# Cross-attention's transposes: from TensorE to 32x32 blocks on VectorE and a round trip through device memory, with a two-step pipeline and doubled projection weights

## What is computed

```python
x = x + _L0_attn_ref(_layernorm(x), ...)                 # causal self-attention, 32 heads of 16
x = x + _L0_xattn_ref(_layernorm(x), ctx_4096, ...)      # cross-attention, below
x = x + _L0_ffn_ref(_layernorm(x), ...)                  # 512x512 linear, 4-bit weights, bias
```

```python
# cross-attention: 32 query heads and 8 key/value heads of width 128; kv_len = 256
kv = jnp.concatenate([context, latents], axis=1)
q = rms_norm((latents @ Wq)..., q_norm_w); k = rms_norm((kv @ Wk)..., k_norm_w); v = (kv @ Wv)...
scores = jnp.einsum('bhgqd,bhkd->bhgqk', qg, k) * scale
probs = jax.nn.softmax(scores, axis=-1)
out = jnp.einsum('bhgqk,bhkd->bhgqd', probs, v)
return out.reshape(...) @ Wo
```

## Time and profile before

| | |
|---|---|
| median of three runs | 1114.6 us |
| the profiled execution's own time | 1114.33 us |
| its span in the trace (first to last instruction) | 1112.2 us |
| TensorE matmuls busy | 1050.4 us (94%) |
| VectorE, ScalarE, GpSimd busy | 757.1, 611.9, 358.5 us |
| mean granted TensorE clock | 0.982 of full |
| bytes moved by DMA | 31.73 MB, mean 29 GB/s |

### The profile page before, as it was taken

One profiled execution on the slowest core, in us unless ns is written; L12 is line 12 of the kernel. 1 busy time (PEld: TensorE's weight loads), 2 busy tenths in 40 slices (PEclk: granted clock), 3 DMA queues, 4 the chain that ended last, 5 costly groups with the idle time before them and its releaser, 6 DMA issues.

```text
span 1112.2 us, 19358 instructions
## 1 busy us (share of the span) xinstructions
PE 1050.4 (94%) x6436; PEld 902.8 (81%) x6436; DVE 757.1 (68%) x1561; ACT 611.9 (55%) x2324; POOL 358.5 (32%) x460
## 2 busy tenths in 40 slices
PE   6788888778999999999999999999999999999998
PEld 5666666547888888888888888888888888888886
DVE  6788888756557756665666576657666665667774
ACT  2666666525555655555555555555555555555551
POOL 4622333033114312431432143114313331433443
PEclk9899999878999999999999999999999999999999
DMA  5000010003001100110011011001100110010002
GB/s 180 21 10 9 9 66 10 1 3 126 6 1 58 39 1 2 57 38 0 19 38 38 0 57 38 0 0 57 38 0 0 57 38 0 11 37 1 1 1 76
DMA packets 8935, 31.73 MB, mean 29 GB/s; under 512 B 1600, under 2 KB 1600, under 8 KB 6720
## 3 DMA queue, kind: packets, MB, share of 16 engines
q1 hardware_dynamic: 8896, 31.23, 8.0%
HBM read 29.13 MB, written 2.10 MB: 28 GB/s over the span
## 4 chain that ended last, share of the span: by engine, by line
PE 64%; POOL 7%; DVE 3%; ACT 2%; issue 1%; POOLq 0%; DVEq 0%
PE ps_q L76 15%; PE ps_y L76 14%; PE ps_kv L76 13%; PE ps_s L76 7%; PE ps_o L76 7%; PE ps_pT L1210 4%; POOL wq_lo L876 3%; POOL wkv_lo L876 2%; PE ps_q L1216 2%; ACT p L957 1%; PE ps_kv L1221 1%; POOL q_rms L884 1%; DVE neg_max L1042 1%; POOL k_rms L884 1%; DVE wkv_hi L1035 0%
## 5 line engine op out<-in xcount | busy, mean ns | idle before, releaser
L957 ACT ACTIVATE p<-ps_s,bias,q_rms 128x256 f32<-128x256 f32 x256 | 141.3, 560 | 117.1 <-DVE bias L1046 116.3
L1068 DVE TENSOR_TENSOR pT_lo<-ps_pT,pT_hi 128x512 fp32r<-128x512 f32 x128 | 82.5, 686 | 75.6 <-ACT pT_hi L983 75.4
L993 ACT ACTIVATE oT_hi<-ps_o 128x512 fp32r<-128x512 f32 x64 | 38.3, 598 | 139.2 <-PE ps_o L76 139.2
L882 POOL TENSOR_TENSOR k_rms<-k_mean,rms_eps 128x2 f32<-128x2 f32 x64 | 19.6, 306 | 283.9 <-ACT k_squares L964 283.9
L76 PE MATMUL ps_y<-wo_hi,oT_hi 128*128 128x512 f32 x256 | 106.5, 416 | 0.0
L76 PE MATMUL ps_q<-wq_hi,xT_hi 128*128 128x512 f32 x256 | 101.1, 395 | 2.5 <-POOL wq_lo L876 2.5
L76 PE MATMUL ps_q<-wq_hi,xT_lo 128*128 128x512 f32 x256 | 101.9, 398 | 0.0
L76 PE MATMUL ps_y<-wo_hi,oT_lo 128*128 128x512 f32 x256 | 101.4, 396 | 0.0
L76 PE MATMUL ps_q<-wq_lo,xT_hi 128*128 128x512 f32 x256 | 100.9, 394 | 0.0
L76 PE MATMUL ps_y<-wo_lo,oT_hi 128*128 128x512 f32 x256 | 100.7, 393 | 0.0
L971 ACT ACTIVATE q_sb<-ps_q 128x512 f32<-128x512 f32 x64 | 38.3, 599 | 100.8 <-PE ps_q L76 99.5
(11 more groups left out here) (210 smaller groups left out, 3316.1 us busy)
## 6 DMA issues: line engine op xcount, KB each, us to landing
raw_wq<-in_x_wq SPq DMA_DIRECT2D x8, 1024.0 KB, 4.8
raw_wo<-in_x_wo SPq DMA_DIRECT2D x8, 1024.0 KB, 4.9
raw_wkv<-in_x_wkv SPq DMA_DIRECT2D x8, 512.0 KB, 3.3
ctx_raw<-in_ctxT SPq DMA_DIRECT2D x8, 256.0 KB, 2.6
out<-raw_wq SPq DMA_DIRECT2D x8, 256.0 KB, 2.0
x<-in_x SPq DMA_DIRECT2D x1, 1536.0 KB, 9.8
raw_wq<-in_a_wq SPq DMA_DIRECT2D x2, 512.0 KB, 6.0
raw_wq<-in_a_wo SPq DMA_DIRECT2D x1, 1024.0 KB, 4.7
```

The source lines that it names most:

```text
L957: act.activation(p[:, g, :], ps_s[g // 2][:, g % 2 * KV:(g % 2 + 1) * KV], ACT.Exp, bias=bias[:, g:g + 1], scale=q_rms[:, g:g + 1], accum_ ...
L993: act.activation(oT[0][:], ps_o[:].rearrange("p (g s) -> p g s", g=XG), ACT.Copy).then_inc(o_hi, 1)
L1068: dve.tensor_tensor(pT[1][:, t], ps_pT[t][:].rearrange("p (g s) -> p g s", g=XG), f32(pT[0][:, t]), ALU.subtract).then_inc(pT_lo, 1)
```

## The change

- TensorE no longer transposes `p`, `q` and `k`. VectorE transposes them by blocks of 32x32 (`p_blocks`, `qk_blocks`), SyncE stores the blocks to a scratch tensor in device memory and loads them back with the blocks in their places (`qk_raw`, `pT_raw`): one store and four loads each for queries with keys, and for probabilities. Each of the four loads fills 32 partitions.
- The high halves are then taken from these tiles in SBUF by ScalarE, and the low halves of the queries and of the probabilities by GpSimd (before, VectorE took them). The low half of the keys stays on VectorE.
- The pipeline is deeper: TensorE's step is now `scores(s)`, `project_keys_values(s + 2)`, `project_output(s - 2)`, `project_queries(s + 2)`, `values(s - 1)`.
- `wkv` and `wq` have two pairs of buffers; their splitting is spread over the steps `b = 0` to `5`. Half of `wo_lo` is computed by VectorE in step `b = 1`.
- All 64 steps are written out; there is no loop. The end is ordered anew: rows 0 to 3 of the linear layer run inside the last two steps.

```diff
         def _(sp):
...
+            def queries_keys(s):
+                sp.wait_ge(k_blocked, s + 1)
+                sp.wait_ge(q_blocked, s + 1)
+                wait(sp, qT_lo, s)
+                scratch = io["qk_scratch"][s % 2]
+                sp.dma_start(scratch, qk_blocks[:].rearrange("p j x c -> p (j x c)")).then_inc(qk_stored, 16)
+                wait(sp, kT_lo, s)
+                sp.wait_ge(qk_stored, 16 * (s + 1))
+                quadrants = scratch.rearrange("(i r) (j x) -> j r i x", i=4, j=4)
+                for j in range(4):
+                    sp.dma_start(qk_raw[R * j:R * j + R].rearrange("p i x c -> p i (x c)"), quadrants[j]).then_inc(qk_loaded[s % 4], 16)
+            def probs(s):
+                sp.wait_ge(p_blocked, 2 * s + 2)
...
+                sp.dma_start(scratch, p_blocks[:].rearrange("p m g c -> p (m g c)")).then_inc(p_stored, 16)
...
+                sp.wait_ge(p_stored, 16 * (s + 1))
...
+                for j in range(4):
+                    sp.dma_start(f32(pT_raw[s % 2][R * j:R * j + R].rearrange("p i t x -> p i (t x)")),
+                                 quadrants[j]).then_inc(p_loaded[s % 4], 16)
...
+            for s in range(STEPS):
+                j, b = divmod(s, B)
+                if s + 1 < STEPS:
+                    queries_keys(s + 1)
+                probs(s)
+                if b == 3 and j < LAST:
...
+                    load(raw_wo, "x_wo", wo_in, j + 1)
+                if b == 4 and j + 2 < XKVH:
...
+                    load(raw_wkv, "x_wkv", wkv_in, j + 2)
+                if b == 6 and j + 2 < XKVH:
...
+                    load(raw_wq, "x_wq", wq_in, j + 2)
...
+                if b == 7 and j + 1 == LAST:
+                    for t in range(2):
+                        for g in range(8):
+                            sp.dma_start(scale[16 * g:16 * g + 16, t, :],
...
         def _(pool):
+            def queries_low(s):
+                pool.wait_ge(qT_hi, s + 1)
+                pool.tensor_tensor(qT[1][:].rearrange("p g (i c) -> p g i c", i=4),
+                                   qk_raw[:, :, 0:XG, :].rearrange("p i g c -> p g i c"),
+                                   f32(qT[0][:]).rearrange("p g (i c) -> p g i c", i=4), ALU.subtract).then_inc(qT_lo, 1)
+            def probs_low(s):
+                pool.wait_ge(pT_hi, s + 1)
+                raw = pT_raw[s % 2][:].rearrange("p i t x -> p (i t x)")
+                pool.tensor_tensor(raw, f32(raw), f32(pT_hi_sb[:].rearrange("p i t x -> p (i t x)")),
+                                   ALU.subtract).then_inc(pT_lo, 1)
...
+            for s in range(STEPS):
+                j, b = divmod(s, B)
+                if j < LAST and b in (2, 3):
+                    weights_low(wkv[(j + 1) % 2], raw_wkv, (2 * b - 4, 2 * b - 3), wkv_hi, wkv_lo, j + 1)
+                if j < LAST and b in (4, 5):
+                    weights_low(wq[(j + 1) % 2], raw_wq, (2 * b - 8, 2 * b - 7), wq_hi, wq_lo, j + 1)
+                if s:
+                    probs_low(s - 1)
+                if s + 2 < STEPS:
+                    k_rms_step(s + 2)
+                if s + 1 < STEPS:
+                    queries_low(s + 1)
+                if b == 1:
+                    weights_low(wo, raw_wo, (2, 3), wo_hi, wo_lo, j + 1)
+                if s + 2 < STEPS:
+                    q_rms_step(s + 2)
...
         def _(act):
+            for s in range(STEPS):
+                j, b = divmod(s, B)
+                if s >= 2:
+                    output_high(s - 2)
                 exps(s)
+                if s:
+                    probs_high(s - 1)
+                if s + 2 < STEPS:
+                    keys_values(s + 2)
+                if s + 1 < STEPS:
                     queries_keys_high(s + 1)
+                if s + 2 < STEPS:
+                    query_sums(s + 2)
...
         def _(dve):
+            def probs(s, h):
...
+                wait(dve, p_stored, 16 * s)
+                dve.wait_ge(p_ok, 2 * s + h + 1)
+                dve.transpose(p_blocks[:, :, two, :], p[:, two, :].rearrange("p g (m r) -> p m g r", r=R)).then_inc(p_blocked, 1)
...
+            def queries_blocked(s):
+                dve.wait_ge(q_ps, s + 1)
+                wait(dve, qk_stored, 16 * s)
+                dve.transpose(qk_blocks[:, :, 0:XG, :].rearrange("p j x c -> p x j c"),
+                              ps_q[:].rearrange("p (g j r) -> p g j r", g=XG, r=R)).then_inc(q_blocked, 1)
...
+            for s in range(STEPS):
+                j, b = divmod(s, B)
                 biases(s)
+                if s >= 2:
+                    output_low(s - 2)
+                probs(s, 0)
+                probs(s, 1)
+                if s + 2 < STEPS:
+                    values_low(s + 2)
+                if s >= 2:
+                    residual(s - 2)
+                if b == 1:
+                    output_weights(j)
+                if s + 1 < STEPS:
+                    keys_low(s + 1)
+                if s + 2 < STEPS:
+                    keys_blocked(s + 2)
+                    queries_blocked(s + 2)
```

More of the change, by code:

```diff
@@ L780, in cross_attention_and_linear @@
         p = sb("p", [P, XG, KV])
-        pT = split("pT", [P, 2, XG, S])
+        p_blocks = sb("p_blocks", [P, 8, XG, R])
+        pT_hi_sb = sb("pT_hi_sb", [P, 4, 2, XG * R], F32R)
+        pT_raw = [sb(f"pT_raw{i}", [P, 4, 2, XG * R], F32R) for i in range(2)]
         oT = split("oT", [P, XG, S])
@@ L799, in cross_attention_and_linear @@
         ps_q, ps_kv = mem["ps_q"], mem["ps_kv"]
[L800 removed]
         ps_o, ps_y = ps("ps_o"), ps("ps_y")
[L802 to L803 removed]
+        ps_xn = [ps("ps_xn"), ps_kv]
+        ps_f = [ps("ps_f"), ps_q]
         kv_rows = ps_kv[:].rearrange("p (t w) -> p t w", t=2)
@@ L872, in _, with weights_low @@
         def _(pool):
-            def weights_low(w, raw, hi, lo, count):
+            def weights_low(w, raw, rows, hi, lo, count):
                 pool.wait_ge(hi, count)
-                for c in range(C):
+                for c in rows:
                     i = pool.tensor_tensor(w[1][:, c, :], raw[:, c, :], f32(w[0][:, c, :]), ALU.subtract)
@@ L1174, in _, with project_keys_values @@
+            statistics(6)
+            normalised(6)
+            out_row(4)
+            out_row(5)
+            output_low(STEPS - 1)
+            xn_low_row(6)
+            residual(STEPS - 1)
+            statistics(7)
+            normalised(7)
+            out_row(6)
+            xn_low_row(7)
+            out_row(7)
         @block.tensor
         def _(pe):
-            def project_keys_values(s, b, j):
-                wait(pe, kT_lo, s)
-                if not (isinstance(j, int) and j == 0):
-                    pe.wait_ge(wkv_lo, j)
-                rows = slice(b * S, (b + 1) * S)
+            def project_keys_values(s):
+                j, b = divmod(s, B)
+                wait(pe, v_lo, s)
+                wait(pe, k_ok, s)
+                wait(pe, wkv_lo, 2 * j)
+                rows, weight = slice(b * S, (b + 1) * S), wkv[j % 2]
@@ L1298, in build @@
+            xn_transposed(4)
+            xn_transposed(5)
+            project_output(STEPS - 2)
+            linear(4)
+            linear(5)
+            values(STEPS - 1)
+            xn_transposed(6)
+            project_output(STEPS - 1)
+            linear(6)
+            xn_transposed(7)
+            linear(7)
 def build(nc, io):
```

502 lines of the change are left out of this document (236 added, 266 removed).

## The result

The kernel after takes 1157.65 us, median of four runs (1145.42 to 1161.73); the kernel before took 1114.49 us beside it. The ratio is 1.037 (95% interval 1.029 to 1.046): slower, 98 us above the forecast and outside its range. The profiled execution took 1155.22 us, its span 1153.4 us.

The account below looks back on a forecast made before the run. TensorE's own work was taken as the bound, 12.86 us a step. 1114.3 - 101.7 = 1012.6 us, plus 16 + 7 + 6 + 4 + 10 + 4, gave 1059.6, so 1060 us; range 1022 to 1130.

Parts of the forecast that it names:

- The floor of a step: TensorE's own work in a plain step once the transposes go: 12.86 - 1.56 = 11.30 us.
- The four plain chains: GpSimd scores to scores, probabilities, queries and keys, SyncE: each closes within 11.3 us in plain steps, within 2 us of it.
- The weights: Weight loads queued ahead of a store of queries and keys: one us a head, +7 us (0 to 50).
- Rival 4: TensorE's clock drops after waits of 1 to 3 us; 22.6 us a step at half clock; 0.18 with rival 2.
- rival 1: Divisions caught by `probs_low` on GpSimd, weight loads then come through in full: 1118 us (1085 to 1145); chance 0.23.
- 0.1 us of margin: In a plain step the last division starts at 5.3 us, `probs_low` at 5.3 to 5.4, so the division may go first.
- GpSimd's weights against `bias` and divisions in steps 2 to 5, 28 times: GpSimd's weight work holding up VectorE in these steps: +4 us (0 to 15).
- rival 2: SyncE's stores and loads through device memory bound the step, 14 us: 1233 us; decides from 12.1; 0.18 with Rival 4.
- Last head and tail: GpSimd's unpacking, linear layer waiting in the last two steps, last row alone: +10 us (0 to 20).
- the loads of `scale`: Sixteen small loads issued in one step ahead of the next step's queries: 7.4 us of issue less slack, +6 us.
- step `b = 1`: VectorE splits `wo` ahead of `kT_lo`, eight times: step 13.1 instead of 11.3 us, +16 us (0 to 25).

Follow-up runs that it names:

- run 5: Kernel after without most of the later heads' weight loads (stale weights) and without the division of the probabilities: 1063.95 us, ratio 0.955.
- run 1: Kernel after with later heads' weight loads fetching only 64 columns (stale weights), all engine work kept: 1104.93 us, ratio 0.993.
- run 2: Kernel after without VectorE's division of the probabilities by their sums: 1111.26 us, ratio 0.999.
- run 7: Kernel after with all eight rows of the linear layer moved behind the last step: 1140.88 us, ratio 1.023.
- run 9: Kernel after with weights loaded in quarters, scale loads four a step, GpSimd waiting for the divisions and the linear layer last: 1090.43 us, ratio 0.980.
- run 13: As run 9, but the weight quarters are issued by ScalarE into its own queue: 1079.92 us, ratio 0.967.
- run 11: Kernel after with probabilities transposed on TensorE again, weights in quarters and the linear layer last: 1085.60 us, ratio 0.974.

## Why the prediction was wrong, by its steps

**The floor was right.** "The floor of a step is 11.30 us" measured 11.28 in run 5, the transposition 0.71 (taken 0.69), the store of the probabilities 2.7 (2.8), doubled weights 2.8 (2.5). Scores of step 2 start at 285.6 (forecast 287). The four plain chains of the forecast hold within 11.3 us when nothing irregular happens, with the divisions too: step 6 takes 11.3 us in the kernel after, steps 7 and 0 do in run 1.

**The weights: the step that failed first.** "1 MB at 351 GB/s is 3.0 us: the chain of 20 to 21 becomes 23 to 24. One us for a head, 7." Measured 53 (run 1), 7.8 us a head. The rate was the mean of all transfers of the kernel before (31.23 MB in 8.0% of the span); in the window at 618 the stream moved 181 GB/s, in part in pieces of 768 B and 1 KB. The store behind `wo` lands in 7.7 us; the forecast had 2.4 + 3.0. It had left out the four loads of the probabilities issued just ahead: from 618.00 on 0.5 + 1 + 0.375 MB are under way, landed at 628.84. And behind the wait the clock is low: scores 2.93 instead of 1.42 us, keys and values 4.15 instead of 2.88, 2.8 us more at this place. Rival 4 came nearest to this, with waits in each step, and I gave it no price of its own. The forecast's own bound for this term was "0 to 50", just short of what was measured.

**The divisions: the second step that failed, and not where rival 1 had it.** Rival 1, with a chance of 0.23, gave pairs of 2 to 3 us (2.67 and 2.87) and scores waiting for `qT_lo` in steps 4, 5 and 7 (16.5, 13.8, 13.9), and these came. But it expected the catch in plain steps, where the forecast had "0.1 us of margin", and there the good side came out. The rows of a plain step, head 3, `b = 7`:

```profile
664.94 0.62 DVE L1132 TENSOR_SCALAR p<-p,inv 128x256 f32<-128x256 f32 x2
```

```profile
665.32 2.51 POOL L940 TENSOR_TENSOR pT_raw<-pT_raw,pT_hi_sb 128x1024 fp32r<-128x1024 f32 x1 [3.22 <-ACT pT_hi_sb L1045]
```

`probs_low` starts 0.1 us behind the start of the last division, and the pair takes 0.62. Counted over heads 1 to 6 of the kernel after, a division of over 0.6 us (one alone takes 0.31 to 0.39) stands in none of the 18 steps `b = 1, 6, 7`, in 22 of the 24 steps `b = 2` to `5`, and in four of the six `b = 0`, which follow the long step 7; in run 1 it is 21 of the same 24 and none of all others. In `b = 2` to `5` GpSimd has the next head's weights ahead of `probs_low`; they hold up VectorE first (the pair at 597.83, beside them, takes 1.14 us) and change which of the two starts earlier. So the term that was mis-sized is "GpSimd's weights against `bias` and divisions in steps 2 to 5, 28 times: +4. (0 to 15.)": it had no layout of such a step, with `probs_low` behind the weights. Run 1 against run 5 puts the divisions at 41 us with no weights to load, a little of it VectorE's own dividing. No run moves GpSimd's weights elsewhere, so their part is read from these counts and not tested. That a margin of 0.1 us held in every plain step is luck; the layout, summed from durations of other instructions, was not that exact.

The time of rival 1, 1118, was 40 too low, because of its link between the two causes: it let the divisions cost something only by using up the slack of the weights. Run 2 against run 5 shows the weights at 47 us with no division in the way. Its 7.5 us of weights a head, where 7.8 were measured, agree by luck as well: they were reckoned at the full rate and clock. In rival 2 a subtraction is off, 47 us over 64 steps leave 0.8 of the 1.56 and not 0.7; its threshold of 12.1 us is right.

The Trainium skill ("SBUF — State Buffer", section "SBUF: two separate sides") has the exclusive lock that was cited. The traces agree again: 681 ns a division with a free order, 418 with GpSimd held back.

**Last head and tail, +10 us: the third.** From the scores of step 56 to the end the kernel before takes 132.7 us. Without the 11.8 us of transposes in it, and 1.5 less for the deeper pipeline (5.7 - 4.2), that is a floor of 119.4; the forecast adds 6 for the loads of `scale`, 2 for `b = 1` and 10. Measured are 159.6 us in run 5 and 166.3 in the kernel after. In run 5, where heads are bare, the seven steps of head 7 still take 103.3 us, against 79.1 for seven of 11.3. Step 56, with the loads of `scale`, has 6.7 of the 24 (a term of its own in the forecast, 6: right); step 57 3.3, step 60 3.0, and step 62, with the linear layer inside, 11.2. So the term of 10 measures some 33 in run 5 and 40 in the kernel after, where its upper bound was 20. Run 7 gives back 17 by order alone. That "the linear layer waits inside the last two steps" was right in kind; its 4 us were too few. What the other half of the term is, no run shows.

**Too high:** step `b = 1`, 2.0 us taken, 0.6 measured (11.9), 5 us instead of 16. Most of the splitting of `wo` was hidden after all. GpSimd's weights against `bias` alone cost nothing in run 5, whose steps 2 to 5 take 11.3 to 11.4 us; against the divisions they do, as said.

**Rival 2** did not decide in the kernel after (SyncE waits 8.7 us at most, and the chain is mixed), but it is the next bound: 12.5 us a step in run 9.

The sum, by stretches of the span, which the forecast puts at 1057.5 (1059.6 less the 2.1 outside it): 287 to the scores of step 2, about 633 from there to step 56 (54 x 11.3, and 12, 7 and 4 us of its terms), 137 from there to the end. Measured are 285.6, 701.6 and 166.3. The middle is 68 us over: run 5 has 614.8 there, 18 under the forecast, and the 86.8 on top are 43 for the weights alone (run 2 less run 5), 35 for the divisions alone (run 1 less run 5), and 9 that come only with both. The end is 29 over. Together -1 + 68 + 29 = 96, and the profiled execution is 95.6 over the forecast.

How much of this is the low clock by itself stays open, for no run was made; the windows of the middle stretch, of the kernel after and then of run 5, bound it:

```profile
285.56:987.18 701.62, 640.90 (x3564) 555.10 (x3564) 539.36 (x1052) 365.52 (x1350) 396.91 (x394) 0.96 0.53 167
285.73:900.53 614.80, 611.90 (x3565) 536.39 (x3565) 419.37 (x836) 362.67 (x1350) 399.88 (x394) 1.00 0.52 164
```

TensorE is idle for 60.7 us in the first and 2.9 in the second, and busy 29 us longer with the same matmuls. At a clock of 0.96 over 701.6 us some 28 us of work are lost at most (an estimate: 0.04 x 701.6). So two thirds of the 86.8 us are the waits and up to a third is the clock behind them. Also open is why run 13 falls between its two theories, 3 us below that of the bytes.

## What to carry to other kernels

Work taken from the bound engine is worth what the next chain leaves: here a step could close at 11.3 us, but three loads of weights, subtractions on GpSimd that catch VectorE's divisions, and a reordered end each cost more than the slack, and more than the 99 us of transposes came back as waits and as a low clock. Lay out the irregular steps as carefully as the plain one: the plain one was right to 0.1 us, and the loss was in the others. Where a chain waits for a transfer in every step, price the irregular transfers by all the bytes in flight at that moment, not by the rate of one alone, and cut them into pieces per step. Most of the loss was a matter of order and not of the idea: with its weights loaded in quarters, GpSimd waiting and the linear layer last, the whole change is 2.0% faster than before instead of 3.7% slower (run 9), 3.3% with the quarters in ScalarE's queue (run 13). With only queries and keys by the round trip it is 2.6% (run 11), with a chain that is TensorE's alone; half of this change is worth about as much as all of it.
